# A graph network's first hop: counts as the moving operand, sums kept by feature

## The reference, cut to what matters

```
m = (x @ W2 + h_bias)[src] * edge_weight          # layer 3
x = layernorm(x + segment_sum(m, dst))

norm = dinv[src] * dinv[dst]                      # layer 4; dinv = 1/sqrt(degree), loops included
h = x
for _ in range(3):
    h = segment_sum(norm[:, None] * h[src], dst)  # edges and self loops
x = layernorm(x + h @ W3 + b3)
```

## Time and profile before

| | |
|---|---|
| median of 3 runs | 7859.46 us (7859.25 to 7867.06) |
| the profiled execution's own span | 9014.9 us (no time beside the span is given) |
| instructions recorded | 163525 |
| mean granted TensorE clock | 0.777 |

### The profile page before, as it was taken

The page is one execution under the profiler, slowest core; times in us unless marked ns, Lnnn a source line. Parts: engine busy times, 40 slices in busy tenths (PEclk is TensorE's granted clock), DMA queues, the critical chain, the costliest instruction groups (busy, mean ns, idle before and its releaser), DMA issues.

```text
span 9014.9 us, 163525 instructions
## 1 busy us (share of the span) xinstructions
PE 5434.1 (60%) x62971; PEld 4715.0 (52%) x62971; DVE 2921.7 (32%) x5181; ACT 1301.5 (14%) x1613; POOL 3562.5 (40%) x3543
## 2 busy tenths in 40 slices
PE   6999889933333333333652455544555455799999
PEld 6999779922222222222542344433444344799998
DVE  6999521111111111112863323332332332311111
ACT  4777510000000000000750000000000000000000
POOL 2111000056666666666725555555555555000000
PEclk9999899966666666666985666666666766899999
DMA  4444268733333332333831222222222222688887
GB/s 129 183 182 182 86 218 254 247 78 81 87 82 81 82 82 76 82 82 98 251 97 35 56 73 73 75 70 70 73 73 74 76 73 76 196 276 268 264 259 229
DMA packets 559779, 1155.29 MB, mean 128 GB/s; under 512 B 155247, under 2 KB 367217, under 8 KB 546465
## 3 DMA queue, kind: packets, MB, share of 16 engines
q1 hardware_dynamic: 234784, 794.54, 27.5%
q10 hardware_dynamic: 215616, 239.17, 8.2%
q0 software_dynamic: 108896, 114.33, 6.5%
HBM read 898.83 MB, written 248.88 MB: 127 GB/s over the span
## 4 chain that ended last, share of the span: by engine, by line
PE 36%; issue 26%; another core or an unknown queue 15%; DVE 5%; ACT 2%; POOL 1%; DVEq 1%; DMA 1%; ACTq 0%; POOLq 0%; SPq 0%; PEldq 0%
PE banks L859 18%; PE banks L953 10%; PE banks L963 5%; POOL gath L366 1%; DVE oneh L1014 1%; DVE area L1836 1%; DVE area L1894 1%; ACT gath L1383 1%; DVE oneh L1845 1%; ACT banks L1380 1%; PE banks L552 1%; PE banks L540 1%; PE banks L1543 1%; PE banks L1552 0%
## 5 line engine op out<-in xcount | busy, mean ns | idle before, releaser
L366 POOL DMA_INDIRECT gath<-tab_l,idx x3328 | 3145.1, 945 | 3296.1 <-DMA idx<-src_idx 1131.6
L1552 PE MATMUL banks<-area,ones 128*128 128x448 f32 (+1 forms) x1040 | 604.9, 752 | 1248.1 <-DVE area L1836 1050.8
L953 PE MATMUL banks<-area 128*128 128x128 f16 x4802 | 575.4, 247 | 894.6 <-issue 893.9
L1552 PEld LDWEIGHTS banks<-area,ones 128*128 128x128 f32 x1040 | 284.5, 285 | 1536.2 <-issue 1522.1
L953 PEld LDWEIGHTS banks<-area 128*128 128x128 fp8e4 x4802 | 356.6, 107 | 1095.2 <-issue 1091.2
L963 PE MATMUL banks<-oneh,gath 128*64 128x128 f32 x3328 | 581.2, 353 | 411.9 <-DMA gath<-tab_l,idx 349.8
L1836 DVE TENSOR_TENSOR area<-gath,banks 128x448 f32<-128x448 f32 (+1 forms) x256 | 138.6, 583 | 1992.2 <-remote 1194.1
L963 PEld LDWEIGHTS banks<-oneh,gath 128*64 128x64 f32 x3328 | 544.7, 188 | 439.0 <-DMA gath<-tab_l,idx 355.6
L825 ACT CAST wide<-banks 128x784 uint16<-128x784 f32 x784 | 651.5, 859 | 221.9 <-PE banks L782 221.9
L794 PE MATMUL banks<-feat,wide 128*128 128x129 f16 x9604 | 670.6, 220 | 0.3 <-ACT wide L825 0.3
L794 PEld LDWEIGHTS banks<-feat,wide 128*128 128x128 fp8e4 x9604 | 606.2, 97 | 0.5 <-issue 0.5
(11 more groups left out here) (257 smaller groups left out, 6169.2 us busy)
## 6 DMA issues: line engine op xcount, KB each, us to landing
gath<-counts SPq DMA_DIRECT2D x294, 784.0 KB, 4.5
oneh<-counts SPq DMA_DIRECT2D x294, 784.0 KB, 4.5
counts<-wide SPq DMA_DIRECT2D x98, 1568.0 KB, 5.2
gath<-counts ACTq DMA_DIRECT2D x98, 784.0 KB
area<-counts ACTq DMA_DIRECT2D x98, 784.0 KB
area<-edge_feat SPq DMA_DIRECT2D x128, 448.0 KB
gath<-tab_l,idx POOLq DMA_INDIRECT x3328
edge_h<-area ACTq DMA_DIRECT2D x128, 416.0 KB
```

The source lines that it names most:

```text
L366: pool.indirect_dma_start(out=to[:, h, c, 0:H], out_offset=None, in_=table[:, :], in_offset=bass.IndirectOffsetOnAxis(ap=idx[:, slot, c:c ...
L953: last = T.matmul(to, part_in[u].bitcast(f8)[:, t, s * P:(s + 1) * P], block_rows[:, k % 2, s, :, :].rearrange("p a f -> p (a f)"), start= ...
L1552: ins = T.matmul(bank[n][:, 0:(hi - lo) * H], ones[:, :], src[:, lo:hi, :].rearrange("p c f -> p (c f)"), start=first and lo == 0, stop=la ...
```

## The change

The parts of the first hop swap the operands of their products. Now the block's rows are stationary (128 sources x 128 numbers, half and feature) and the counts move: for each of the 7 source tiles one product of 512 and one of 384 columns, 14 in all, whose result is [(half, feature), node]. The sums of the hop are kept in that form, one tile of 128 x 12544 numbers in `wide`, and each part is added with one operation of 128x896. The edge weights move from `wide` to `area` to make room. The own rows of a block no longer go through `parts[0]`; they are added by seven products with the identity (`own_product`) and one more addition, behind the block's last part (for the last block ahead of its first). In the last block the sums of each destination block are turned back by seven float32 products (`sums_by_node`), which add the two halves too, and the result is scaled from PSUM (`scaled_by_node`). VectorE scales part j after it has added part j+2. ScalarE's loop over the last block's parts keeps its order.

```diff
-        att_s = wide[:, NP - GROUPS * C:NP].rearrange("p (g c) -> p g c", c=C)
...
+        att_s = area[:, 2 * BN:2 * BN + GROUPS * C].rearrange("p (g c) -> p g c", c=C)
...
-        FEW = 10
-        sums_a, sums_b = wide[:, NT * H:NT * H + FEW * TB * H], area[:, 2 * BN:2 * BN + (NB - FEW) * TB * H]
+        hop_sums = wide[:, 0:NP]
...
+        def part_load(act, b, j, last_block=False):
+            m = part_number(b, j, last_block)
+            hold(act, c_mm, m + 2 if j >= 2 else m if last_block else m + 1)
             act.dma_start(part_in[j % 2], counts[j * TB:(j + 1) * TB, :, bass.ds(b * BW, BW)]
                           .rearrange("t p n -> p t n")).then_inc(c_in[j % 2], 16)
...
         def early_act(act, b, k, groups):
-            part_load(act, b, 0)
-            part_load(act, b, 1)
+            last_block = k == EARLY
+            part_load(act, b, 0, last_block)
+            part_load(act, b, 1, last_block)
             hold(act, p_att.added, groups + 2)
-            l2_steps(act, b, [(1, sums_to_sta), *ln_act(4), (11, keep_resid), (15, keep_block(k))])
+            l2_steps(act, b, [(1, sums_to_sta), *ln_act(4), (11, keep_resid)])
             for j in range(NB):
                 if j + 2 < NB:
-                    part_load(act, b, j + 2)
-                if k == EARLY:
+                    part_load(act, b, j + 2, last_block)
+                if last_block:
                     act.wait_ge(f_sc, j + 1)
                     S.copy(tiles(parts_of(1, 0), j), nod[:, j % 2, 0, :, :]).then_inc(f_hi, 1)
...
         def part_product(pe, b, k, j, last_block=False):
-            n, u = NB * b + j, j % 2
+            m, u = part_number(b, j, last_block), j % 2
             hold(pe, c_in[u], 16 * (NB // 2 * b + j // 2 + 1))
-            hold(pe, c_ev, 2 * n + 1)
-            hold(pe, l_turn, L2_STEPS * b + (16 if last_block else 15))
+            hold(pe, c_ev, m + 2 if j == 0 and not last_block else m + 1)
+            hold(pe, l_turn, L2_STEPS * b + 15)
+            for s in range(TB):
+                for lo, hi in ((0, 4), (4, TB)):
+                    last = T.matmul(two_banks(u, 1)[:, lo * P:hi * P].rearrange("p (t n) -> p t n", n=P), features_of(k, s),
+                                    part_in[u].bitcast(f8)[:, lo:hi, s * P:(s + 1) * P],
+                                    start=(s == 0), stop=(s == TB - 1))
+            last.then_inc(c_mm, 1)
...
+        def own_product(pe, b, k, last_block=False):
+            m, u = part_number(b, -1 if last_block else NB, last_block), 1 if last_block else 0
+            hold(pe, c_ev, m + 1)
+            hold(pe, l_turn, L2_STEPS * b + 15)
+            for s in range(TB):
+                last = T.matmul(two_banks(u, 1)[:, s * P:(s + 1) * P], features_of(k, s), ident_h[:, 1, :],
+                                start=True, stop=True)
+            last.then_inc(c_mm, 1)
+        def sums_by_node(pe, j):
+            pe.wait_ge(c_ev, part_number(EARLY, j, True) + 3)
+            if j >= 2:
+                pe.wait_ge(f_sc, j - 1)
             for t in range(TB):
-                to = two_banks(u, 1)[:, t * P:(t + 1) * P]
-                if last_block:
-
-                    T.matmul(to, ident_h[:, 1, :], parts[0][:, j * TB + t, :, :].rearrange("p a f -> p (a f)"),
-                             start=True, stop=False)
-                for s in range(TB):
-                    last = T.matmul(to, part_in[u].bitcast(f8)[:, t, s * P:(s + 1) * P],
-                                    block_rows[:, k % 2, s, :, :].rearrange("p a f -> p (a f)"),
-                                    start=(s == 0 and not last_block), stop=(s == TB - 1))
-            last.then_inc(c_mm, 1)
+                last = T.matmul(bank[7 * (j % 2)][:, t * H:(t + 1) * H], hop_sums[:, (j * TB + t) * P:(j * TB + t + 1) * P],
+                                w_norm[:, 0, :], start=True, stop=True)
+            last.then_inc(f_turn, 1)
...
+                if st == NB // 2:
+                    own_product(pe, b, k)
...
             step(EARLY, EARLY, 0)
+            own_product(pe, EARLY, EARLY, last_block=True)
             for j in range(NB):
                 part_product(pe, EARLY, EARLY, j, last_block=True)
+                if j > 0:
+                    sums_by_node(pe, j - 1)
                 if j == NB - 2:
-                    pe.wait_ge(c_mm, NB * EARLY + j + 3)
+                    pe.wait_ge(c_mm, part_number(EARLY, j, True) + 4)
                     pe.sem_inc(h_mm[1], 3)
+            sums_by_node(pe, NB - 1)
...
+            def added(m, u, at):
+                hold(dve, c_mm, m + 4)
+                hold(dve, c_ev, m + 1)
+                V.tensor_tensor(hop_sums[:, at], hop_sums[:, at], two_banks(u, 1), ALU.add).then_inc(c_ev, 1)
+            def part_added(b, j, last_block=False):
+                added(part_number(b, j, last_block), j % 2, slice(j * BN, (j + 1) * BN))
...
+                if st == NB // 2:
+                    added(part_number(b, NB), 0, bass.ds(b * BN, BN))
...
+            V.memset(hop_sums, 0.0).then_inc(s_pre, 1)
...
-            for j in range(NB):
-                part_added(EARLY, j)
-                dve.wait_ge(c_ev, 2 * (NB * EARLY + j) + 5)
+            def scaled_by_node(j):
+                dve.wait_ge(f_turn, j + 1)
                 if j >= 2:
                     dve.wait_ge(f_lo, j - 1)
-                V.scalar_tensor_tensor(nod[:, j % 2, 0, :, :], hop_sums(j), 1.0 / COUNT_UNIT, by_tile(dinv2, j), ALU.mult,
-                                       ALU.mult).then_inc(f_sc, 1)
+                V.scalar_tensor_tensor(nod[:, j % 2, 0, :, :],
+                                       bank[7 * (j % 2)][:, 0:TB * H].rearrange("p (t f) -> p t f", f=H),
+                                       1.0 / COUNT_UNIT, by_tile(dinv2, j), ALU.mult, ALU.mult).then_inc(f_sc, 1)
                 if j > 0:
                     to_parts(j - 1)
+            added(part_number(EARLY, -1, True), 1, slice(EARLY * BN, (EARLY + 1) * BN))
+            for j in range(NB):
+                part_added(EARLY, j, last_block=True)
+                if j > 1:
+                    scaled_by_node(j - 2)
+            scaled_by_node(NB - 2)
+            scaled_by_node(NB - 1)
             to_parts(NB - 1)
```

More of the change, by code:

```diff
@@ L287, in gnn_program @@
         c_in, c_mm, c_ev = p_hop[0].rows_in, sem("part_product"), sem("part_half_added")
+        f_turn = sem("first_hop_by_node")
         f_sc, f_hi, f_lo = sem("first_hop_scaled"), sem("first_hop_high"), sem("first_hop_low")
@@ L902, in parts_of @@
             return parts[k][:, :, a, :]
-        L2_STEPS = 15
+        L2_STEPS = 14
+        PARTS = NB + 1
         def l2_steps(eng, b, steps):
@@ L909, in l2_steps, with part_number @@
                 work(b, 1).then_inc(l_turn, 1)
-        def part_load(act, b, j):
-            n = NB * b + j
-            hold(act, c_mm, n + 1)
+        def part_number(b, j, last_block=False):
+            return PARTS * b + j + (1 if last_block else 0)
+        def part_load(act, b, j, last_block=False):
+            m = part_number(b, j, last_block)
+            hold(act, c_mm, m + 2 if j >= 2 else m if last_block else m + 1)
             act.dma_start(part_in[j % 2], counts[j * TB:(j + 1) * TB, :, bass.ds(b * BW, BW)]
@@ L933, in early_act, with features_of @@
             for j in range(NB):
                 if j + 2 < NB:
[L935 to L936 removed]
+                    part_load(act, b, j + 2, last_block)
+                if last_block:
                     act.wait_ge(f_sc, j + 1)
                     S.copy(tiles(parts_of(1, 0), j), nod[:, j % 2, 0, :, :]).then_inc(f_hi, 1)
+        def features_of(k, s):
+            return block_rows[:, k % 2, s, :, :].rearrange("p a f -> p (a f)")
         def part_product(pe, b, k, j, last_block=False):
[L942 removed]
+            m, u = part_number(b, j, last_block), j % 2
@@ L967, in early_pe @@
             pe.sem_inc(p_att.summed, RING)
-            pe.sem_inc(c_mm, 2)
+            pe.sem_inc(c_mm, 3)
             pe.sem_inc(l_turn, 1)
@@ L1004, in early_dve @@
             dve.sem_inc(p_att.added, 2)
-            dve.sem_inc(c_ev, 3)
+            dve.sem_inc(c_ev, 2)
             def place(q, h):
@@ L1044, in step @@
                         part_added(b, j)
+                if st == NB // 2:
+                    added(part_number(b, NB), 0, bass.ds(b * BN, BN))
             for q in range(2):
                 place(q, q)
-            V.memset(sums_a, 0.0).then_inc(s_pre, 1)
-            V.memset(sums_b, 0.0).then_inc(s_pre, 1)
-            dve.wait_ge(s_pre, 9)
+            V.memset(hop_sums, 0.0).then_inc(s_pre, 1)
+            dve.wait_ge(s_pre, 8)
             with dve.Fori(0, BEFORE // 2) as i:
```

13 lines of the change are left out of this document (removed).

## The result

| | median us | runs | against before |
|---|---|---|---|
| before | 7859.35 | 4 (7853.27 to 7867.06) | |
| after | 7952.18 | 4 (7942.41 to 7962.90) | 1.0116, 95% interval 1.0102 to 1.0131 |

The change makes the kernel 93 us slower; forecast were 84. The profiled execution of the changed kernel is one of the timed ones (span 7961.1 us), unlike that of before, whose 9014.9 us stood far off its runs. So the comparison needs a profile of before that is one of its usual executions. The kernel before was therefore profiled once more, unchanged.

A forecast was written before the change was run, and what follows sets the result against it. GpSimd's nearly back-to-back gathers (16.2 us a group) were taken to bound the gather stage, adding 0 us; the last block behind them, its loads in series, added 84: 7859.5 + 84 = 7943 us, range 7915 to 7965.

The forecast's parts named there:

- The cause and the sign: Last block: ScalarE's loads queue behind casts that wait for product j+2, so loads run in series; slower by 84 us.
- three signs named: Last block's profile: products 10.4 to 13.5 us apart, loads about 0.9 us behind casts, block 130 to 170 us.
- The turn: Last block, parts 3 to 13: load, product, addition, scaling and cast in series, 7.94 us and a 4.2 us product, 12.1 us.
- The last load: Last block, part 13: like every load in series, 5.0 us from its issue until the product starts.
- The end: End of the last block: addition, turning, two scalings, cast and subtraction, 5.9 us.
- The term of the last block: Path behind the last gather: ends at 7864.4 against 7780.7, +84 us.
- Gather stage: Parts 0 to 181: products and additions lie beside the gathers, 2.7 us a part at full clock, so 0 us.
- Rival 1: Gather stage: GpSimd's stalls are at least partly in the runs and vanish with fewer TensorE records, 7661 us; chance 0.19.
- my own reading of the stalls: GpSimd's 1198.8 us of waits come from recording, as TensorE instructions retire late while gathers run; absent from the runs.
- Rival 2: Last block: ScalarE's queue hands loads out ahead of the cast's wait, no series, 7852 to 7862 us; chance 0.07.
- Rival 3: Gather stage gets longer: TensorE work of 16.7 us over 16.2 of gathers, 7 us or 120 us (8070); chance 0.06.

The follow-up runs named there:

- before again: The kernel before, unchanged, profiled once more for an execution that is one of its usual ones; 7869.12 us.
- four slots: The kernel before, with the last block's part loads going to four slots in place of two (two more in the one-hot buffer); 7851.15 us, ratio 0.9978.

## Why the prediction was right, and where it was off

- **The cause and the sign.** Right and shown from both sides: the order alone, put into the old form, costs 95 us; casts moved later or loads moved to another program give all of it back. Of the three signs named, the block's time (154.9 us for 130 to 170) and the loads behind casts came. Products came 11.2 to 12.6 us apart, inside 10.4 to 13.5, but for the first pair, 9.9 (6575.21 to 6585.15), and the last, 15.3 (6692.43 to 6707.77).
- **The turn.** Forecast 12.1 us, measured 11.89, but by two errors that cancel. From cast to load I took 0.90 us from the earlier trace rows; it is 0.09. There the load waits for the product that frees its slot, not for the cast (in before again the cast is at 6567.48, that product's last seven start at 6567.71 for 0.55 us, the load is at 6568.38): the row was right, its reading was not. The other way, product and clock were worse than 4.2 us: the fixed steps of the turn above are 0.26 + 1.01 + 0.65 + 0.09 + 4.89 = 6.90 us, which leaves 4.99 us for the product (the ten rows from part 3 to part 12 have 4.27 to 5.39, 4.86 on the mean; some loads took a little over 4.89), at a clock of 0.72.
- **The last load** took 8.9 us in place of 5.0. SyncE's loads for the second hop were issued just before it, at 6697.06 to 6698.35. That it shared the DMA with them is the likely reason, which no run tests; I had not looked at what is issued near it. The end, from the last product's to the last subtraction's, took 5.7 us (5.9 forecast).
- **The term of the last block.** 152.6 us forecast (7711.8 to 7864.4), 154.9 measured. But it was set against the 68.7 us of one odd execution; before again takes 74.5. TensorE's granted clock was 0.90 in the one and 0.83 in the other, and the same products keep it busy for 51.6 and for 56.6 us (7712 to 7780, 6560 to 6634). So the block is +80.5 and not +84. With the 8.4 us of the second hop, which no step of mine had, that makes 88.9 of the 93.8 between the two spans; the other 5 are within what executions vary by. The mechanism was right, but that the total came within 9 us is in part luck.
- **Gather stage.** Right at nothing: a part takes 2.81 us, 14 products start to turning 2.65 us, which is 54 ns for 128 columns. It goes by columns, and not by the 1.8 us (an estimate) that follow from the 131 ns for 512 columns in the Trainium skill ("TensorE: Matmul & The Clock Gate", Back-to-back issue gap).
- **Rival 1** (stalls also in the runs) is refuted by before again. But so is my own reading of the stalls, that each TensorE record delays the engine, and with it the detail that a profile with fewer TensorE records would be shorter by hundreds of us: the same records, no stalls. **Rival 2** is refuted by the loads, each of which follows its cast by 0.09 us; its time, 7852 to 7862, is about that of the kernel with SyncE's loads (7862.76). **Rival 3** would have needed more than twice the products.

## What to carry to other kernels

When a result is consumed later, go through each program that waits for it and ask what is queued behind that wait: a lag of two parts on VectorE cost nothing by itself (a last block of 64.7 us with the loads in SyncE's program) and some 80 us through ScalarE's program, because the loads stood behind the cast. A DMA issue belongs ahead of waits that it doesn't need, or in a program that has none. And where a change alters the number of an engine's instructions, look at the turns of the long loops behind it before you explain the last 0.1%: here the same code 96 instructions further on took 9 us less in one loop and 9 more in the next.

## What the runs showed of the hardware that I had not expected

- The place of a loop's code on TensorE is worth 8 to 9 us in six turns (71 against 80 us), with no other change.
- With four slots, a third and a fourth DMA issue from ScalarE's queue, 0.5 us behind the second, took 3.93 us together, and ScalarE's next instruction waited for them. Issued 11.6 us after the second they took 0.99 us.
- One execution of the kernel before took 9014.9 us, with TensorE's sums late in front of gathers; another with the same instructions took 7867.3. What made it so stays open.
- Semaphore increments on TensorE are not free: they come 0.15 us apart (38.0 us for 256). Beginning in 7.8 us of idling, 96 of them made it 13.3 us and 256 made it 38.0.
